# Four small moves in the order of a four-layer gated cross-attention kernel, and one reduction moved into another stretch

## What is computed

```
x = x + tanh(g_xattn[n]) * xattn_n(layernorm(x), ctx)
x = x + tanh(g_ffn[n])   * ffn_n(layernorm(x))
```

```
scores = einsum('bhsr,bhlr->bhsl', q_r, k_r)
attn = softmax(scores, axis=-1)
ctx_c = einsum('bhsl,bld->bhsd', attn, kv_rope)
out = einsum('bhsd,hkd->bshk', ctx_c, w_kc_kv).reshape(b, s, H*K) @ Wo.T
```

## Time and profile before

| | us |
|---|---|
| median of 3 runs (lowest, highest) | 2128.64 (2125.79, 2129.28) |
| the profiled execution's own time | 2128.17 |
| its span, first to last instruction | 2126.4 |
| PE busy | 2040.6, 96% of the span |
| DVE busy | 1485.2, 70% |
| POOL busy | 1359.4, 64% |
| ACT busy | 1074.6, 51% |
| mean granted TensorE clock | 0.994 of full |

### The profile page before, as it was taken

One profiled execution on the slowest core, in us unless ns is written; L12 is line 12 of the kernel. 1 busy time (PEld: TensorE's weight loads), 2 busy tenths in 40 slices (PEclk: granted clock), 3 DMA queues, 4 the chain that ended last, 5 costly groups with the idle time before them and its releaser, 6 DMA issues.

```text
span 2126.4 us, 35215 instructions
## 1 busy us (share of the span) xinstructions
PE 2040.6 (96%) x13564; PEld 1422.9 (67%) x13568; DVE 1485.2 (70%) x2141; ACT 1074.6 (51%) x1770; POOL 1359.4 (64%) x850
## 2 busy tenths in 40 slices
PE   7998999999999998999999999999999999999998
PEld 5787777765565556766555655588897655655588
DVE  6869871588888857666788888653335888888653
ACT  4552332565665656211665665544434656656543
POOL 0368873188788785454788788634441887887644
PEclk9999999999999999999999999999999999999999
DMA  3035776423223104102223222025533232231022
GB/s 99 11 119 178 248 240 202 96 59 88 59 59 88 45 31 140 26 1 63 59 64 83 59 64 68 22 79 156 149 91 78 59 88 59 59 88 45 33 54 72
DMA packets 65704, 179.59 MB, mean 84 GB/s; under 512 B 11280, under 2 KB 21280, under 8 KB 65154
## 3 DMA queue, kind: packets, MB, share of 16 engines
q1 hardware_dynamic: 65154, 177.01, 31.5%
q10 hardware_dynamic: 384, 0.33, 0.1%
HBM read 162.32 MB, written 14.98 MB: 83 GB/s over the span
## 4 chain that ended last, share of the span: by engine, by line
PE 80%; DVE 7%; ACT 5%; POOL 3%; issue 3%; DMA 1%; POOLq 0%; DVEq 0%; SPq 0%; ACTq 0%
PE psum L962 20%; PE psum L1551 19%; PE psum L1537 18%; PE psum L1425 5%; PE psum L1436 3%; ACT E L2011 3%; PE psum L976 3%; PE psum L1709 3%; PE psum L1568 2%; PE psum L1666 2%; PE psum L1354 1%; POOL CL L2030 1%; PE psum L1252 1%; PE psum L1232 1%; DVE ST L2826 1%
## 5 line engine op out<-in xcount | busy, mean ns | idle before, releaser
L2563 DVE TENSOR_REDUCE mx<-psum 128x2 f32<-128x1000 f32 (+1 forms) x540 | 552.5, 1066 | 164.2 <-PE psum L1425 161.7
L2292 POOL TENSOR_TENSOR SA<-SA,E 125x896 f32<-125x896 f32 x288 | 606.3, 2105 | 19.0
L2011 ACT ACTIVATE E<-psum 125x896 f32<-125x896 f32 x576 | 512.7, 918 | 101.2 <-PE psum L1537 83.2
L1551 PE MATMUL psum<-E,V 125*64 125x448 f32 x2304 | 449.4, 539 | 0.0
L1551 PEld LDWEIGHTS psum<-E,V 125*64 125x64 f32 x2304 | 163.4, 137 | 246.4 <-issue 239.0
L1537 PE MATMUL psum<-QH,KH 64*125 64x448 f32 x1152 | 255.3, 399 | 10.2 <-ACT E L2011 4.2
L1537 PE MATMUL psum<-QL,KH 64*125 64x448 f32 x1152 | 241.4, 365 | 0.0
L2292 POOL TENSOR_TENSOR SA<-E,E 125x896 f32<-125x896 f32 x48 | 101.5, 2115 | 200.3 <-PE psum L1425 152.1
L1537 PE MATMUL psum<-QH,KL 64*125 64x448 f32 x1152 | 228.1, 363 | 0.0
L1425 PE MATMUL psum<-KH,QH 64*128 64x500 f32 x864 | 182.0, 405 | 1.8 <-ACT QR L1953 1.6
L2585 DVE RECIPROCAL RS<-psum 128x448 f32<-128x448 f32 x48 | 142.0, 2957 | 46.0 <-PE psum L1568 45.5
(11 more groups left out here) (310 smaller groups left out, 4302.1 us busy)
## 6 DMA issues: line engine op xcount, KB each, us to landing
KH<-kt_scratch SPq DMA_DIRECT2D x96, 375.0 KB, 5.3
KL<-kt_scratch SPq DMA_DIRECT2D x96, 375.0 KB, 7.1
EW<-in_f_w SPq DMA_DIRECT2D x64, 256.0 KB, 5.9
kt_scratch<-kt SPq DMA_DIRECT2D x16, 750.0 KB, 6.4
WS<-in_f_w SPq DMA_DIRECT2D x31, 384.0 KB, 4.7
GB<-gates_scratch SPq DMA_DIRECT2D x36, 224.0 KB, 3.8
slot_of_t<-slots_scratch SPq DMA_DIRECT2D x64, 112.0 KB, 4.4
WoT<-in_a_WoT SPq DMA_DIRECT2D x24, 256.0 KB, 3.4
```

The lines of the kernel that those rows point to most:

```text
L1551: i = e.matmul(psum[c * DC:(c + 1) * DC, 4, 0:HT], V[0:LP, b, tile * DC:(tile + 1) * DC], E[g[n, b, k] % NE][0:LP, half[c]], start=k == 0, ...
L2011: e.activation(E[m % NE][0:LP, :].rearrange("p (c q) -> p c q", c=2), psum[0:LP, pair:pair + 2, 0:HT], ACT.Exp).then_inc(exp_set.sem, 1)
L2292: e.tensor_tensor(SA[b % 2][0:LP, :], a[0:LP, :], x[0:LP, :], ALU.add).then_inc(sum_set.sem, 1)
L2563: e.tensor_reduce(o, psum[:, max_banks(kind, *t), 0:CW], AX.X, ALU.max).then_inc(small_free.sem, 1)
```

## The change

1. In `sparse_order` the first combination of each group stands behind the second half of the next group's gathering, no longer ahead of it.
2. In `core_order` the first pair of maxima products of a batch moves, for batches 2 to 15, from the head of the scores stretch of the batch before to behind value tile 7 of the batch before that. DVE's list moves with it. That is 14 of 16 batches in each of three layers, 42 places.
3. In layer 3's projection the turning stands 3 instead of 4 tiles behind, the logits 5 instead of 6, and the steps of the RMS norm on DVE and POOL one tile earlier.
4. In layers 1 to 3 the products of projection tile 0 stand ahead of the barrier, in bank 6 of PSUM instead of 0.
5. In layer 2's experts ACT's copy (silu) of the third block's first half stands ahead of the first gate, no longer behind it.

```diff
--- before.py
+++ after.py
@@ -258,8 +258,8 @@
         pick = lambda q: [("pick", q)] + ([("pload", q + 3)] if q + 3 < E0 // 2 else [])
         steps = [([("gsl", 0)] if g == 0 else []) + [("ups", g)] + (pick(0) if g == 0 else []), pick(q) if g > 0 else [("gturn", 0)],
                  [("comb", q - 1)] if g > 0 else [], ([("disp", g + 1, 0)] if more else []) + st(0) + (pick(1) if g == 0 else []),
-                 [("downs", q), ("downs", q + 1)], (pick(q + 1) if g > 0 else []) + st(1), [("comb", q)],
-                 ([("disp", g + 1, 1)] if more else []) + st(2), [("downs", q + 2), ("downs", q + 3)],
+                 [("downs", q), ("downs", q + 1)], (pick(q + 1) if g > 0 else []) + st(1),
+                 ([("disp", g + 1, 1)] if more else []) + st(2), [("comb", q)], [("downs", q + 2), ("downs", q + 3)],
                  pick(q + 2), [("comb", q + 1)] + st(3),
                  [("gsl", g + 1)] if more else [], pick(q + 3), [("comb", q + 2)] + ([("gturn", g + 1)] if more else [])]
         for n, step in enumerate(steps):
@@ -305,7 +305,7 @@
             order.append(("load_lows", b + 1))
         following = b + 1 < B
         for k in range(NL):
-            order += [("max", b + 1, *MAX_AT[k])] if following and k in MAX_AT else []
+            order += [("max", b + 1, *MAX_AT[k])] if following and k in MAX_AT and (k > 0 or b == 0) else []
             order.append(("head", b, k))
             order += [("low_end", b + 1, 0)] if following and k == 7 else []
             order.append(("scores", b, k))
@@ -324,6 +324,8 @@
                 order += [("high", b + 2), ("diag", b + 2)]
             if k == 4 and following:
                 order.append(("max_spread", b + 1))
+            if k == 7 and b + 2 < B:
+                order.append(("max", b + 2, 0, 0))
             if k == 8:
                 order += [("div", b - 1)] if b > 0 else []
                 order += [("total", b)] if b == B - 1 else []
@@ -397,10 +399,10 @@
     return [t for t in CORES[n] if n != 2 or not ahead(t)]
 
 
-TURN_BEHIND = {0: 2, 1: 0, 2: 2, 3: 4}
+TURN_BEHIND = {0: 2, 1: 0, 2: 2, 3: 3}
 SPLIT_AT = {0: 3, 2: 1, 3: 1}
 EARLY_UP = {2: 5, 3: 4}
-LOGITS_BEHIND = {0: 2, 1: 0, 2: 3, 3: 6}
+LOGITS_BEHIND = {0: 2, 1: 0, 2: 3, 3: 5}
 TURNED_NORM = {0: 1, 2: 5, 3: 8}
 MADE = (slice(0, 3 * P), slice(3 * P, T))
 BACK = {0: ((0, 1), (2,)), 1: ((3, 4), (5, 6))}
@@ -1572,14 +1574,8 @@
     def pe_project(e, n):
         behind = TURN_BEHIND[n]
         for i in range(NT + LOGITS_BEHIND[n]):
-            if i < NT:
-                e.wait_ge(*low_flag(n, i).at(n, i))
-                if i >= 3:
-                    e.wait_ge(*x_out.at(n, i - 3))
-                pairs = []
-                for m in range(H // 2):
-                    pairs += split_pairs(CH[i % 3][:, m, :], CL[i % 3][:, m, :], MH[:, m, :], ML[:, m, :])
-                product(e, psum[:, i % 3, 0:D], pairs).then_inc(projected.sem, 1)
+            if (1 if n > 0 else 0) <= i < NT:
+                pe_project_tile(e, n, i)
             if behind and 0 <= i - behind < NT:
                 pe_project_turn(e, n, i - behind)
             if n in (2, 3) and i >= LOGITS_BEHIND[n]:
@@ -1587,6 +1583,19 @@
             if n in (2, 3) and i - behind == EARLY_UP[n]:
                 e.wait_ge(*yl_set.at(TURNED_NORM[n], 3))
                 pe_up(e, n, 0, 0)
+
+    def project_bank(n, i):
+
+        return 6 if n > 0 and i == 0 else i % 3
+
+    def pe_project_tile(e, n, i):
+        e.wait_ge(*low_flag(n, i).at(n, i))
+        if i >= 3 and (n == 0 or i > 3):
+            e.wait_ge(*x_out.at(n, i - 3))
+        pairs = []
+        for m in range(H // 2):
+            pairs += split_pairs(CH[i % 3][:, m, :], CL[i % 3][:, m, :], MH[:, m, :], ML[:, m, :])
+        product(e, psum[:, project_bank(n, i), 0:D], pairs).then_inc(projected.sem, 1)
 
     def pe_project_turn(e, n, i):
         r = TURNED_NORM[n]
@@ -1825,6 +1834,7 @@
             else:
                 pe_core(e, n, behind_rope(n, lambda t: t in first_maxima(PRODUCTS_AHEAD)))
             if n > 0:
+                pe_project_tile(e, n, 0)
                 stage_end(e, next(met))
             pe_project(e, n)
             pe_stage_end(e, next(met), 3 if n < 2 else 6, (5, 22, 6, 5)[n])
@@ -2100,11 +2110,13 @@
                 if t[0] >= 2:
                     act_split(e, f, t[0])
             elif kind == "up":
-                if not swiglu or t != [0, 0]:
+                if not swiglu or t != [0, 0] and (f, t) != (2, [2, 0]):
                     act_up(e, f, *t)
             elif kind == "gate":
                 n, c = t
                 x = 2 * n + c
+                if (f, x) == (2, 0):
+                    act_up(e, f, 2, 0)
                 if not swiglu:
                     e.wait_ge(*r_set.at(f, n, c))
                     if x >= 4:
@@ -2310,9 +2322,9 @@
             pool_scales(e, 1 + 2 * n, i)
             if n != 1 and i - SPLIT_AT[n] in (0, 1):
                 pool_split(e, n, i - SPLIT_AT[n])
-            if n == 3 and i >= 2:
-                pool_rms(e, i - 2)
-        for i in (NT - 2, NT - 1) if n == 3 else ():
+            if n == 3 and i >= 1:
+                pool_rms(e, i - 1)
+        for i in (NT - 1,) if n == 3 else ():
             pool_rms(e, i)
 
     def pool_rms(e, i):
@@ -2625,7 +2637,7 @@
                 low_part(e, n, i + 2)
             if i < NT:
                 e.wait_ge(*projected.at(n, i))
-                e.scalar_tensor_tensor(X[:, i, :], psum[:, i % 3, 0:D], tanh_g[:, n:n + 1], X[:, i, :], ALU.mult,
+                e.scalar_tensor_tensor(X[:, i, :], psum[:, project_bank(n, i), 0:D], tanh_g[:, n:n + 1], X[:, i, :], ALU.mult,
                                        ALU.add).then_inc(x_out.sem, 1)
                 e.wait_ge(*x_out.at(n, i))
                 dve_stats(e, r, i)
@@ -2652,17 +2664,17 @@
     def dve_rms(e, k):
 
         m = ffn[3]
-        i = k - 2
+        i = k - 1
         if 0 <= i < NT:
             e.wait_ge(*sq_set.at(i))
             e.tensor_scalar(m["rr"][:, i:i + 1], m["ss"][:, i:i + 1], 1.0 / D, 1e-6, ALU.mult, ALU.add).then_inc(ms_set.sem, 1)
-        i = k - 3
+        i = k - 2
         if i == 0:
             e.wait_ge(*rms_in_w.at())
         if 0 <= i < NT:
             e.wait_ge(*rms_set.at(i))
             e.scalar_tensor_tensor(Y[:, i, :], Y[:, i, :], m["rr"][:, i:i + 1], m["rw"][:, :], ALU.mult, ALU.mult).then_inc(z_set.sem, 1)
-        i = k - 5
+        i = k - 4
         if i >= 0:
             dve_turn(e, 8, i, 4 + i % 4)
```

## The result

The kernel with the change takes 2147.94 us (median of 3 runs, 2145.5 to 2148.3) against 2128.64: a ratio of 1.0097, with a 95% interval from 1.0079 to 1.0114. It is 19.3 us slower, where 10.3 were forecast; the sign was right and the size was not, and the time lies 1.9 us above the range.

The account below looks back on a forecast made before the run. PE was taken to bound the kernel, busy 2040.6 of 2126.4 us. The terms, -6.5 + 15.8 + 4.3 - 1.3 - 2.0 = +10.3 us on 2128.17, gave 2138.5 us, with a range of 2127 to 2146.

Parts of the forecast that it names:

- A: Layer 0's experts: combinations behind the gathering fill PE's seven waits for YDL, -6.5 us (-8 to -2).
- B: Cores: the pair of maxima among value tiles costs 0.60 us, saves 0.22 at the head, 42 times: +15.8 us.
- C: Layer 3's projection: norm steps a tile earlier shorten PE's 3.0 us wait for a normed tile, -1.3 us (-3 to 0).
- D: Layers 1 to 3: projection tile 0 ahead of the barrier opens it 1.4 us later each time, +4.3 us (+2 to +6.5).
- E: Layer 2's experts: the early copy removes PE's 2.36 us wait, -2.0 us (-3.4 to -1).
- The other five come to about 6 us: Layer 0's experts: gain from the YDL waits after the first two, which POOL's selection limits to 0.3 us.
- The lower end of 2 us: Layer 0's experts: least gain, from the waits of the last two groups, where the context's work has ended.
- The waits for maxima: Scores stretch: PE's 135 waits, 38.7 us, stay; the rival that they shrink gives 2120.5 us, chance 0.05.
- the division: Rival in the cores: DVE divides late, delaying ACT's eviction of the sums, 0.2 us a batch, 2147 us, chance 0.04.
- the one of equal price: Rival in the cores: the pair of maxima costs the same in both places, 2122.7 us, chance 0.09.
- 0.1 for clock: Barriers of layers 1 to 3: 0.1 us for lower clock, added to three delays of 1.4 us.
- So the down product starts about 1.7 us earlier: Layer 2's experts: with the early copy, HL from POOL is next late; 0.3 us more for clock.

Follow-up runs that it names:

- A alone: Kernel before with only the first combinations moved behind the second half of the next gathering: 2127.41 us against 2127.65, ratio 1.0001.
- B alone: Kernel before with only the first pair of maxima moved behind value tile 7: 2142.47 us against 2127.65, ratio 1.0073.
- C with E: Kernel before with only layer 3's earlier norm steps and layer 2's early copy: 2127.89 us against 2127.65, ratio 0.9999.
- D alone: Kernel before with only projection tile 0 ahead of the barrier in layers 1 to 3: 2133.63 us against 2127.65, ratio 1.0038.
- the f32 probe: Kernel before plus one unused plain f32 matmul of 500 columns, 128x64, between value tiles 7 and 8: batch 23.58 us against 22.76.

## Why the prediction was right and wrong

| term | forecast | measured | by |
|---|---|---|---|
| A | -6.5 (-8 to -2) | 0 (-1.7 to +2.1) | A alone |
| B | +15.8 (0 to 17.6) | +14.15; +15.5 (13.0 to 18.3) alone | batches; B alone |
| C | -1.3 (-3 to 0) | -1.1 | trace of C with E |
| D | +4.3 (+2 to +6.5) | +6 to +8 | D alone, trace and runs |
| E | -2.0 (-3.4 to -1) | -0.7 to +0.7, within scatter | two traces |

**A failed**, and with it two thirds of the error of 9.4 us. The step was "The other five come to about 6 us": of a chain of five engines only POOL was asked whether it could keep up. PE also turns the context's keys in that stretch, which ACT, DVE and a transfer must take away, and ACT waited 7.3 us for this transfer even before. Speeding PE up there only moved the wait (22.8 us of ACT's waits for the transfer). The row at hand that should have raised the question is the transfers' share of 0.77 and 0.81 in the earlier trace rows. The lower end of 2 us was not an end either, since it assumed the last two groups free.

**B held**, mechanism and size: 0.335 us a batch against 0.38, since the pair in the values stretch costs 0.57 and not 0.60, and its removal saves 0.24 and not 0.22. The waits for maxima stayed, the division was not late, and so those two rivals and the one of equal price fell. What was wrong is the reason given for the price. Value tiles are not only of full height, but split by columns and of another type. The products of the earlier trace rows differ from the pair in form alone. That they gave nearly the right number (0.62 - 0.22 = 0.40, where 0.35 was measured) was luck: a change of form and type at once costs no more than one of them.

**D was mis-sized**: the barriers were right (3.6 for 4.2), the "0.1 for clock" measured about 3.4 us in part D's trace. With A it makes most of the error. The waits of 3.8, 2.6 and 2.6 us were forecast as 2.4 to 3.7; I had named a stretch at 1.2 GHz as the high end only.

**E failed** behind "So the down product starts about 1.7 us earlier": it does, by 1.9, but the term took this lead for the gain, and what comes late next was asked once and not twice. Behind HL came ML, 1.92 us late, from DVE, which the copy does not feed, and what is left cannot be told from 0.

**C held.** With it the wait for the normed tile fell from 2.99 to 2.14 us. The signs for the steps came out as listed (batch of 23.1, YDL for S, CL waits, no R), but for the waits for kt, which the list did not have. The value products around the pair are 0.90 us apart (0.38 + 0.10 + 0.42), not 0.97.

## What to carry to other kernels

Before crediting a removed wait, list every resource that the waiting engine feeds or drains in that stretch, the buffers of outgoing transfers too, and ask each whether it has slack: here A was worth nothing until one more buffer freed the transfer, and with it the two gave 6 to 7 us. Do not put a matmul of another form or another operand type into a run of matmuls; group such products, since the cost (0.30 to 0.35 us here) is paid once per group. A wait that makes PE idle behind a barrier costs more than its length when the granted clock falls behind it (7.0 us here, where the barriers opened 3.6 us later). Compare the mean granted clock of two kernels before crediting a difference of a few us to a mechanism.

## What was unexpected of the hardware

- A change of operand type, plain f32 to fp32r, in the same form broke PE's flow for 0.30 us, almost as much as a change of form (0.35), and the two together cost 0.35, not the sum.
- Plain f32 products are recorded as two passes: 0.23 us for an idle product of 128 columns, 0.84 us for one of 500.
- Two value products with 64 columns each start 7 ns apart and run side by side. One single product of this form and type among them (the f32 probe) costs its full 0.84 us, though value passes of the other half start 7 to 9 ns behind its two passes: the price comes at the end of the stretch, where the last two passes of its own half (487.64 and 488.01 us) run alone.
- With the same instructions ahead of it, layer 1's first value product came between 431.1 and 437.3 us in fourteen traces. Most of this goes with the granted clock: ahead of it PE was at the lower level (1.2 GHz) for 6.8 us in the earliest and 17.1 us in the latest of them, and 10.2 us in the trace of before (432.9). A gain of 2 us in that stretch needs many runs or the offsets of single instructions, not two spans.
